# Gate logits of a mixture-of-experts layer as eight f32 products in place of 24 products of f16 halves

## What is computed

```python
xn = layernorm(x)
x = x + sparse_linear(xn) + linear_attention(xn)      # 16 heads, then W_out
t = rmsnorm(layernorm(x)) * norm_scale                # [1250, 1024]
logits = t @ gate_w + gate_b                          # gate_w [1024, 8]
top_v, top_i = top_k(logits, 2); probs = softmax(top_v)
x = x + layernorm(x) + sum over the two experts of probs * expert(t)
```

## Time and profile before

| | |
|---|---|
| median of 3 runs | 1120.47 us (1119.83 to 1121.78) |
| the profiled execution | 1117.66 us |
| its span, first to last instruction | 1115.9 us |
| mean granted clock of TensorE | 0.936 of full speed |
| busy: TensorE / VectorE / ScalarE / GpSimd | 948.5 / 758.8 / 302.0 / 195.0 us |
| mixing stage with gate | about 524 to 821 us |
| routing | about 821 to 841 us |
| experts | about 841 to 1116 us |

### The profile page before, as it was taken

The page is one execution under the profiler, slowest core; times in us unless marked ns, Lnnn a source line. Parts: engine busy times, 40 slices in busy tenths (PEclk is TensorE's granted clock), DMA queues, the critical chain, the costliest instruction groups (busy, mean ns, idle before and its releaser), DMA issues.

```text
span 1115.9 us, 18538 instructions
## 1 busy us (share of the span) xinstructions
PE 948.5 (85%) x5609; PEld 590.9 (53%) x5610; DVE 758.8 (68%) x1231; ACT 302.0 (27%) x502; POOL 195.0 (17%) x220
## 2 busy tenths in 40 slices
PE   2526999999999989999788999999726989999993
PEld 1323666666666655555555666666524545555551
DVE  4889788888888889722777777776564545555551
ACT  0561222222222222533111121211101323333331
POOL 1133000000000010000323232223102233243321
PEclk9757899999999999999889999999957999999997
DMA  7544544333343331493135443535536996977553
GB/s 242 158 141 144 215 151 150 139 124 124 139 150 141 141 132 39 114 316 101 55 95 168 123 146 124 162 99 174 170 135 235 310 302 148 314 204 211 118 105 57
DMA packets 77814, 176.17 MB, mean 158 GB/s; under 512 B 24180, under 2 KB 39482, under 8 KB 73922
## 3 DMA queue, kind: packets, MB, share of 16 engines
q1 hardware_dynamic: 70001, 147.40, 39.3%
q0 software_dynamic: 7776, 28.32, 11.3%
HBM read 113.54 MB, written 62.67 MB: 158 GB/s over the span
## 4 chain that ended last, share of the span: by engine, by line
PE 21%; DVE 13%; DMA 8%; issue 6%; ACT 2%; POOL 1%; SPq 1%; DVEq 0%; POOLq 0%; ACTq 0%
PE windows L946 8%; PE bank L838 5%; DMA arena<-t_dram,arena 4%; DVE arena L1437 4%; DMA out_x<-arena 3%; PE bank L964 3%; PE bank L937 2%; PE bank L831 1%; PE windows L899 1%; DVE arena L1476 1%; DVE arena L1436 1%; DVE arena L1438 1%; DVE arena L1471 1%; ACT arena L1128 1%; PE windows L838 1%
## 5 line engine op out<-in xcount | busy, mean ns | idle before, releaser
L758 PE MATMUL bank<-arena 128*125 128x512 f16 x960 | 218.6, 385 | 0.0
L838 PE MATMUL bank<-arena 128*125 128x512 f16 x864 | 195.5, 384 | 1.8 <-POOL arena L616 1.8
L758 PEld LDWEIGHTS bank<-arena 128*125 (+1 forms) x960 | 130.0, 139 | 74.0 <-issue 5.1
L838 PEld LDWEIGHTS bank<-arena 128*125 (+1 forms) x864 | 118.5, 138 | 67.4 <-issue 3.0
L946 PE MATMUL windows<-arena 128*128 x648 | 149.4, 381 | 0.0
L814 PE MATMUL bank<-arena 128*128 128x416 f16 (+1 forms) x576 | 103.1, 338 | 0.0
L946 PEld LDWEIGHTS windows<-arena 128*128 128x128 f16 x648 | 63.6, 98 | 65.7 <-issue 1.3
L814 PEld LDWEIGHTS bank<-arena 128*128 128x128 f16 x576 | 55.5, 97 | 44.0
L964 PE MATMUL bank<-arena 128*128 x324 | 74.4, 379 | 2.3 <-DVE arena L1639 2.3
L1332 DVE TENSOR_TENSOR arena<-windows,arena 128x1024 f32 x49 | 59.8, 1220 | 22.1 <-issue 7.7
L616 POOL TENSOR_TENSOR arena<-arena 128x250 f32 (+1 forms) x40 | 27.1, 677 | 265.7 <-ACT arena L1109 265.7
(11 more groups left out here) (227 smaller groups left out, 1421.4 us busy)
## 6 DMA issues: line engine op xcount, KB each, us to landing
arena<-split_dram SPq DMA_DIRECT2D x56, 512.0 KB, 5.1
arena<-in_w_flat SPq DMA_DIRECT2D x22, 1024.0 KB, 6.4
split_dram<-arena SPq DMA_DIRECT2D x44, 512.0 KB, 3.7
arena<-in_w_flat SPq DMA_DIRECT2D x40, 256.0 KB, 3.6
split_dram<-arena SPq DMA_DIRECT2D x80, 128.0 KB, 2.3
arena<-in_x SPq DMA_DIRECT2D x20, 448.0 KB
arena<-in_w_qkv SPq DMA_DIRECT2D x8, 1024.0 KB, 6.4
t_dram<-arena SPq DMA_DIRECT2D x10, 448.0 KB
```

Source lines behind the costliest of these rows:

```text
L758: mm = pe.matmul(bank[b][0:TT, :], xt[:, l, k, tok(i)], wkv[:, r, k, c0:c0 + 512], start=(k == 0 and n == 0), stop=(k == KT - 1 and n == 2))
L838: mm = pe.matmul(o[half][0:TT, :], a_[:, l, k, tok(i)], w_[:, r, k, c0:c0 + 512], start=(m == 0 and k == 0 and c == 0), stop=(m == 1 and k ...
```

## The change

The transposed row stays f32: ScalarE's copy writes f32, and the step that makes the low half (`tt_lo`) goes. The gate weight is used as it was loaded; the two f16 halves, the scale by `SW` and the semaphore for them go. TensorE makes 8 f32 products in place of 24 f16 ones. `tt_done` is now counted up by ScalarE, twice a tile, and TensorE's transposes wait on it.

```diff
-        tt = T([2, KT, TT], F16)
+        tt = T([KT, TT])
...
-        gate_hl = T([2, KT * E], F16)
...
             def gate_tile(i, h):
                 pe.wait_ge(t_ready, i + 1)
+                if not (isinstance(i, int) and i == 0):
+                    pe.wait_ge(tt_done, 2 * i)
...
             def gate_logits(i):
-                pe.wait_ge(tt_done, i + 1)
+                pe.wait_ge(tt_done, 2 * (i + 1))
                 pe.wait_ge(gate_done, START + i)
                 for k in range(KT):
-                    for c, (l, r) in enumerate(((0, 0), (0, 1), (1, 0))):
-                        mm = pe.matmul(bank[6][0:TT, 0:E], tt[:, l, k, :], gate_hl[:, r, k * E:(k + 1) * E],
-                                       start=(k == 0 and c == 0), stop=(k == KT - 1 and c == 2))
+                    mm = pe.matmul(bank[6][0:TT, 0:E], tt[:, k, :], gate_f[:, k * E:(k + 1) * E], start=(k == 0), stop=(k == KT - 1))
                 mm.then_inc(gate_mm, 1)
             gate_tile(0, 0)
-            pe.wait_ge(gate_w_ready, 1)
+            pe.wait_ge(mixc_in, 80)
...
-                    a_.activation(tt[:, 0, 4 * b:4 * b + 4, :], bank[4 + b][:, 0:4 * TT].rearrange("p (k n) -> p k n", n=TT), ACT.Copy).then_inc(tt_hi, 1)
+                    a_.activation(tt[:, 4 * b:4 * b + 4, :], bank[4 + b][:, 0:4 * TT].rearrange("p (k n) -> p k n", n=TT), ACT.Copy).then_inc(tt_done, 1)
...
-            v.wait_ge(mixc_in, 80)
-            st.done(v.tensor_scalar(gate_hl[:, 0, :], gate_f, SW, None, ALU.mult))
-            v.scalar_tensor_tensor(gate_hl[:, 1, :], gate_f, SW, gate_hl[:, 0, :], ALU.mult, ALU.subtract).then_inc(gate_w_ready, 1)
...
-            def tt_lo(i):
-                for b in range(2):
-                    v.wait_ge(tt_hi, 2 * i + b + 1)
-                    ins = v.tensor_tensor(tt[:, 1, 4 * b:4 * b + 4, :], bank[4 + b][:, 0:4 * TT].rearrange("p (k n) -> p k n", n=TT),
-                                          tt[:, 0, 4 * b:4 * b + 4, :], ALU.subtract)
-                ins.then_inc(tt_done, 1)
...
                 gate(i - 2)
-                tt_lo(i - 1)
```

More of the change, by code:

```diff
@@ L266, in build_gps_layer @@
         knw_in = sem("knw_in"); qn_in = sem("qn_in"); qn_ready = sem("qn_ready"); acc_zero = sem("acc_zero")
-        gate_w_ready = sem("gate_w_ready"); t_whole = sem("t_whole");
+        t_whole = sem("t_whole");
         kv_mm = sem("kv_mm"); k_sq = sem("k_sq"); kw_ready = sem("kw_ready"); k_hi = sem("k_hi")
@@ L287, in build_gps_layer @@
         t_out = [sem(f"t_out{h}") for h in range(2)]
-        tt_psum = sem("tt_psum"); tt_hi = sem("tt_hi"); tt_done = sem("tt_done")
+        tt_psum = sem("tt_psum"); tt_done = sem("tt_done")
         gate_mm = sem("gate_mm"); gate_done = sem("gate_done")
@@ L1471, in mix_norm @@
                 v.scalar_tensor_tensor(tm[h][0:TT], xn2[0:TT], tiny[0:TT, 2:3], scale_b[0:TT], ALU.mult, ALU.mult).then_inc(t_ready, 1)
-            def tt_lo(i):
-                for b in range(2):
-                    v.wait_ge(tt_hi, 2 * i + b + 1)
-                    ins = v.tensor_tensor(tt[:, 1, 4 * b:4 * b + 4, :], bank[4 + b][:, 0:4 * TT].rearrange("p (k n) -> p k n", n=TT),
-                                          tt[:, 0, 4 * b:4 * b + 4, :], ALU.subtract)
-                ins.then_inc(tt_done, 1)
             def gate(i):
                 v.wait_ge(gate_mm, START + i + 1)
-                v.scalar_tensor_tensor(logits[0:TT, bass.ds(i, 1), :].rearrange("p a b -> p (a b)"), bank[6][0:TT, 0:E], 1.0 / (ST * SW), gate_bias[0:TT],
+                v.scalar_tensor_tensor(logits[0:TT, bass.ds(i, 1), :].rearrange("p a b -> p (a b)"), bank[6][0:TT, 0:E], 1.0 / ST, gate_bias[0:TT],
                                        ALU.mult, ALU.add).then_inc(gate_done, 1)
@@ L1522, in _ @@
                     add_half(1, 1, j - 4)
-            tt_lo(0)
             mix_norm(1, 0, 1)
@@ L1533, in _ @@
             gate(NT - 2)
-            tt_lo(NT - 1)
             gate(NT - 1)
```

## The result

The changed kernel takes 1108.32 us (median of 4 runs, 1107.46 to 1108.81), the kernel before beside it 1121.12 us (4 runs, 1119.83 to 1124.3): a ratio of 0.9897 with a 95% interval of 0.9879 to 0.9915. It is faster by over 0.2%, as forecast. The profiled execution after took 1108.81 us, with a span of 1107.1.

What follows compares the result with a forecast made beforehand. VectorE's path was taken to set most of the loop's turn, and TensorE to bound it after the change. Gains of 0.30 (first pair), 1.36, 1.39, 2.69 (turns) and 1.64 (last pair) made 7.38 us: 1113.1 us, range 1110 to 1119.

Steps and rivals of the forecast that it cites:

- the bound and where it went: Loop over row-tile pairs: VectorE sets most of the turn now; with its subtractions gone TensorE bounds it; chance 0.50.
- the price of the logits: TensorE's gate logits: 32 passes at today's price, 1.79 us (+0.45) at full clock, 3.63 us (+0.91) at half.
- rival D: Gate logits: 0.213 us an f32 instruction at full clock; 5.2 to 12 us slower, 1125.7 to 1132 us; chance 0.07.
- rival E: Gate logits: 16 instructions at 56 ns, 0.90 us in all; gain near 16.7 us, 1103.8 us; chance 0.05.
- the floor of TensorE's turn: Rolled turns: TensorE's 51.40 us busy plus 0.90 for both logits, 52.30 us; turns one and two gain 1.36 and 1.39.
- the lower clock of turn three: Third rolled turn, 54.99 us: slow stretch of 1.65 us taken as gone with the wait, gaining 2.69 us in all.
- Rival B's first form: The clock dips somewhere all the same: gain 5.7 us, 1114.8 us; chance 0.25 for both forms together.
- Rival B's second form: A late quarter load takes half of VectorE's 1.68 us: turn 52.82, gain 5.8 us, 1114.7 us; chance 0.25 for both forms.
- the last pair: After the rolled turns: addition of tile 9 1.42 us earlier, last logits at half clock; 1.64 us gained in all.
- what the sum was made against: Whole kernel: 7.38 us gain set against the profiled 1117.66 us gives 1110.3; against the runs' median 1120.47, 1113.1.
- Rival C: Expert stage behind the last logits gives the 7 us back by waiting longer for DMA; near 1120.5 us; chance 0.13.

Runs made afterwards that it cites:

- f16_high_only: Changed kernel with 24 f16 products of the high halves in place of the 8 f32 ones, low halves left out; 1106.91 us, ratio 0.9881 to the kernel before.
- after_gate_early: Changed kernel with VectorE's gate of tile 7 put into the middle of the last tile's norm; 1106.82 us, ratio 0.9869 to the kernel before.
- before_fill: Kernel before with eight 512-column products of zeros on TensorE ahead of its wait at each turn's head; 1118.81 us, ratio 0.9977 to the kernel before.
- f32_keep_lo: Kernel before with f32 logits, VectorE's subtractions kept, written to an unread tile and waited for by the logits; 1122.76 us, ratio 1.0025 to the kernel before.
- after_pad: Changed kernel with 48 narrow products and 16 small memsets that nobody needs appended at its end; 1110.46 us, ratio 0.9919 to the kernel before.

## Why the prediction was right, and where it was wrong

**Right: the bound and where it went.** VectorE's path had set the turn, and TensorE sets it now. L1452 follows L1470 by 0.09 us (forecast: within 0.2), VectorE waits 1.10 us for the second logits of a turn (about 1), the wait at the heads of turns two and three is gone but for what a late load leaves (0.82 us at most), and doubling the logits shows their whole price in the turn. The forms of the two parts alone say how it splits: f32 by itself costs 3.3 us, the subtraction moved out of the way gives 6.6.

**Off: the price of the logits.** Forecast 1.79 us from 32 passes at 56 ns; 1.67 measured, so +0.31 us where +0.45 was taken. At the lower clock 3.50 against 3.63. The doubled passes of the 408-column rows were the right reading, and rival D, with 213 ns an instruction at full clock, is ruled out by 104 ns, and so is rival E with 56. The forecast took a pass at what one costs in f16, where each pass has an instruction of its own and 24 of them take 1.36 us from start to start (616.94 to 618.30 in before), 57 ns each. In f32 there are 16 instructions for 32 passes; that this is why a pass comes out cheaper is argued, not shown. The Trainium skill's page "FP8 and Floating Point Precision" (section "Matmul Precision") counts four passes for a true FP32 product; 8 products in 1.67 us are 52 ns a pass by that count. This is near the 57 ns of an f16 pass, so the trace agrees with the count, though not at the same price a pass.

**Wrong: the floor of TensorE's turn.** This is the step of the prediction that failed: the mechanism was right, and the turn that TensorE needs was sized too long, by both of its terms. It was put at 51.40 + 0.90 = 52.30 us, and it measures 51.67. Two times 0.14 us come from the price. The other 0.32 us lie in the 51.40: it was the turn less its two waits, and such a wait is counted from the modelled end of the last product, 5.34 us behind the start of L837's group, while the next group can start 5.18 us behind it (611.61 and 616.79 above). Each wait that goes gives 0.16 us more than it shows. 51.40 - 0.32 = 51.08, and f16_high_only measures 51.06. The waits that are left show the same: the 0.82 us at 657.80 make a stretch 0.99 us longer (52.66 against 51.67), and 0.19 us in after_gate_early make it 0.35 longer (52.02). With both corrections a turn is 0.60 to 0.63 us shorter than forecast; over three turns that is 1.8 us, nearly all of what M to R gave beyond the forecast (9.3 against 7.4). It does not explain the whole miss: with both terms put right the sum is 9.2 us and the forecast 1111.3, and the measured median lies 3.0 us below that. Of these some 1.9 are the open part outside the loop, told below; the rest is within the scatter of the medians.

**Right: the lower clock of turn three is gone.** The stretch T to T that holds its head lasts 55.3 to 55.4 us in all five profiles of before, against 53.6 to 53.7 for the one ahead of it; in none of the six of after is there any such stretch, and before_fill prices it at 1.67 us (1.65 taken). That it went because the wait went fits, but isn't strictly shown: f32_keep_lo keeps the wait of 2.11 us and has no lower clock there either. Rival B's first form is ruled out for turns two and three. At the head of turn one the lower clock stays (four of five profiles of before, five of six of after). Rival B's second form, a quarter that lands late, was seen in turn two, and more often than not: in the six profiles of after ScalarE waits there 2.17, 0.63, 0.82, 1.38, 1.25 and 1.44 us for it, and the stretch T to T is 52.66, 51.67, 51.68, 51.86, 51.74 and 51.93 us. Up to 0.82 us of this wait cost nothing; the longer ones held up the head of the turn by 0.07 to 0.99 us, 0.25 in the mean where B had 0.5 in every turn.

**Close, but by another path: the last pair.** The logits on tile 8 start 2.56 us earlier measured from T (31.19 us behind it, 33.75 before; 2.60 forecast), and from them to the last gate it takes 9.98 us in place of 9.23, 0.75 more where 0.96 was forecast. The sum is 1.81 us in the two first profiles, 2.05 by the means, for 1.64. But the premise that VectorE's own path sets the addition of tile 9 (803.08) "as in a turn" was wrong. In before, this addition stands behind a quarter that lands late; ScalarE, then VectorE:

```profile
801.81 0.63 ACT L1128 ACTIVATE arena<-arena 128x512 f16<-128x512 f32 x1 [5.30 <-DMA arena<-in_w_flat]
...
802.47 0.69 DVE L1486 SCALAR_TENSOR_TENSOR arena<-arena 128x512 f16<-128x512 f32 x1 [5.08 <-ACT arena L1128]
```

In after the same quarter comes 1.71 us earlier from T (L1127 at 793.57), and VectorE is through with it at 794.93, just when TensorE's products end (794.97). Had the load stayed, most of this gain would not have come: the term was right in size by luck. It is also why the last T to R varies in before (43.18 to 43.65) and not in after (41.36 to 41.37).

**Wrong: what the sum was made against.** The profile that I used was the fastest of the five of before: in it alone the head of turn one ran at full clock (M to the first T is 63.38 us, in the other four 65.05 to 65.11). Its stretch M to R was 267.66 us, the mean of five 269.26. Against that one, the first profile of after (260.47, with the lower clock at that head) shows a gain of 7.19 us, which looks like the forecast of 7.38 and is so by two errors that cancel: 1.3 us less than forecast up to the first T, where the clock of that head differs, and 1.1 more behind it (for the most part the floor and the price, less what the late quarter took). To apply the sum to the median was right; its terms were too small.

**Open: 2 us outside the loop.** 1.25 us ahead of M, where the kernel's work is unchanged, and 0.6 behind R make up the rest of the 11.2. They are one and a half times their uncertainty and less. Whether they are chance, I can't say; after_pad and the six further profiles didn't settle it. Rival C, that the stage behind gives the gain back, is ruled out: R comes 9.3 us earlier after M and what lies behind R did not grow.

## What to carry to other kernels

Where a change takes work off the engine that sets a loop, work out the next engine's floor from starts to starts of its groups: here each wait shown was 0.16 us shorter than what its end gave. Take the base of a sum from several profiles when the granted clock varies from one to the next; one stretch at the lower clock was worth 1.7 us here, as much as a term. Splitting an f32 operand into f16 halves has its price on the engines that make the halves: here 24 short products were 0.31 us cheaper than the f32 ones, but the halves kept the turn at 53.65 us by VectorE's path where TensorE's work needs 51.1.

## What was not expected of the hardware

- A run of narrow products can be followed by the lower clock with no wait ahead of it: granted clock 0.64 behind 3.4 us of 8-column f32 products, a group L831 of 1.46 us in place of 0.81 behind 4.1 us of 8-column f16 products. A run of 1.67 us brought none in the rolled turns. The Trainium skill's page "TensorE: Matmul & The Clock Gate" (section "HAM oscillation — how this bites in real kernels") tells of gaps in which TensorE waits; here TensorE is recorded as busy through the whole stretch in which its clock falls.
- A wait does not decide by itself. In before 2.08 us at the head of turn two are followed by the full clock and 2.11 us at turn three by the lower one, in all five profiles; in f32_keep_lo the same 2.11 us are followed by the full clock. What else decides is not settled.
- A narrow f32 product costs 104 ns an instruction, two instructions for each, at full clock, and 211 ns at the lower one (798.28 to 801.66 in after_gate_early, 16 of them). That is the 213 ns of the one-column products in the earlier trace rows, whose stretch has a recorded clock of 1.00; this speaks against the record there, as the prediction held.
